# A decoder layer on one core: new orders on four engines, context remainders on VectorE, early loads of ScalarE's tables

## The reference

```
x = x + linear_attention(layernorm(x))            # 16 heads of 16; q, k -> elu + 1; kv = k^T v; (q kv) / (q sum(k) + 1e-6); o_w, o_b
x = x + softmax(mask(((ctx Wq)(ctx Wk)^T / 8) * layernorm(x)))    # ctx is 256 x 64; the "score" multiplies the normalised x
x = x + W_down(fwht(silu(gate) * up))             # up, gate = W_ug(fwht(layernorm(x))), 1024 wide each, with column scales
```

## Time and profile before

| | |
|---|---|
| three runs | 132.08, 132.26, 132.5 us; median 132.26 us |
| profiled execution, first to last instruction | 130.6 us (the profile gives no other time of its own for this execution) |
| PE busy | 123.9 us, 95% |
| PEld (weight loads, beside PE) | 116.0 us, 89% |
| DVE, ACT, POOL busy | 79.7, 75.4 and 68.8 us |
| granted TensorE clock | 1.000 |

### The profile page before, as it was taken

The page is one execution under the profiler, slowest core; times in us unless marked ns, Lnnn a source line. Parts: engine busy times, 40 slices in busy tenths (PEclk is TensorE's granted clock), DMA queues, the critical chain, the costliest instruction groups (busy, mean ns, idle before and its releaser), DMA issues.

```text
span 130.6 us, 2612 instructions
## 1 busy us (share of the span) xinstructions
PE 123.9 (95%) x974; PEld 116.0 (89%) x974; DVE 79.7 (61%) x202; ACT 75.4 (58%) x162; POOL 68.8 (53%) x89
## 2 busy tenths in 40 slices
PE   6899999996999999999999999999999999999991
PEld 2249799986999999699999999999999999999990
DVE  1279969677997794999786486662535512232211
ACT  1497639984576589668553883556496630345500
POOL 2200999889999998746270344452326350055500
PEclk9999999999999999999999999999999999999999
DMA  4999985000000000000000200000200000200011
GB/s 113 304 346 381 397 241 201 0 0 3 3 5 0 0 0 8 0 0 0 5 0 0 80 0 5 3 0 0 85 0 0 3 0 5 80 0 0 0 39 47
DMA packets 4353, 7.68 MB, mean 59 GB/s; under 512 B 560, under 2 KB 2096, under 8 KB 4212
## 3 DMA queue, kind: packets, MB, share of 16 engines
q1 hardware_dynamic: 4334, 7.50, 17.0%
q10 hardware_dynamic: 6, 0.01, 0.0%
HBM read 6.46 MB, written 1.05 MB: 57 GB/s over the span
## 4 chain that ended last, share of the span: by engine, by line
PE 60%; POOL 13%; DVE 11%; ACT 7%; issue 4%; DMA 3%; POOLq 0%; ACTq 0%
PE bank L1123 31%; PE bank L1136 18%; POOL wd_a L303 4%; POOL wug L309 4%; DMA x_res<-in_x 3%; PE bank L1003 3%; POOL rstd L263 2%; DVE st L644 2%; PE bank L1087 2%; PE bank L1109 2%; PE bank L1025 2%; POOL wd_b L303 2%; PE bank L1069 1%; ACT L518 1%; DVE xT L802 1%
## 5 line engine op out<-in xcount | busy, mean ns | idle before, releaser
L1123 PE MATMUL bank<-xh_home,wug 128*128 128x256 f32 x384 | 49.5, 285 | 0.3 <-DVE at L737 0.3
L1123 PEld LDWEIGHTS bank<-xh_home,wug 128*128 128x128 f32 x384 | 47.1, 191 | 0.9 <-issue 0.7
L314 POOL TENSOR_TENSOR hs<-front,hs 128x256 fp32r<-128x256 f32 x32 | 24.0, 758 | 33.1 <-ACT hs L527 33.1
L518 ACT ACTIVATE front<-bank,vecs 128x256 f32<-128x256 f32 x32 | 15.0, 472 | 20.3 <-PE bank L1123 20.1
L825 DVE SCALAR_TENSOR_TENSOR front<-bank,sc_up,front 128x256 f32<-128x256 f32 x32 | 15.2, 480 | 18.2 <-ACT front L518 18.2
L1136 PE MATMUL bank<-wdh,hs 128*128 128x256 f32 x192 | 23.7, 283 | 0.0
L1136 PEld LDWEIGHTS bank<-wdh,hs 128*128 128x128 f32 x192 | 23.3, 191 | 0.0
L527 ACT CAST hs<-front 128x256 fp32r<-128x256 f32 x32 | 12.8, 400 | 4.0 <-DVE front L825 4.0
L1025 PE MATMUL bank<-wqkv,xT 128*128 128x256 f32 x96 | 14.1, 288 | 0.1
L1025 PEld LDWEIGHTS bank<-wqkv,xT 128*128 128x128 f32 x96 | 12.2, 189 | 1.2 <-ACT xT L436 0.7
L261 POOL TENSOR_SCALAR veps<-mv 128x2 f32<-128x2 f32 x12 | 2.3, 192 | 19.8 <-DVE mv L647 19.1
(11 more groups left out here) (105 smaller groups left out, 194.1 us busy)
## 6 DMA issues: line engine op xcount, KB each, us to landing
wd_a<-in_w_d SPq DMA_DIRECT2D x1, 1024.0 KB, 8.6
front<-in_w_ug SPq DMA_DIRECT2D x2, 512.0 KB, 9.7
back<-in_w_ug SPq DMA_DIRECT2D x2, 512.0 KB, 5.0
out<-x_res SPq DMA_DIRECT2D x8, 128.0 KB, 1.9
wd_b<-in_w_qkv SPq DMA_DIRECT2D x3, 256.0 KB, 4.9
x_res<-in_x SPq DMA_DIRECT2D x1, 512.0 KB, 6.6
x_res<-in_x SPq DMA_DIRECT2D x1, 385.0 KB, 3.8
back<-in_ctx_t SPq DMA_DIRECT2D x1, 260.0 KB
```

The costliest lines, as they stand in the source:

```text
L314: g.tensor_tensor(hs[:, 1, n % JB, :], sg[:, n % RING, :], hs[:, 0, n % JB, :].bitcast(F32), ALU.subtract)\
L518: a.activation(sg[:, n % RING, :], B("GU", n)[:, 0:SEQ], ACT.Silu, scale=vecs[:, V_WSUG + JB + j:V_WSUG + JB + j + 1]).then_inc(s["sg"], 1)
L1123: ins = mm(dst[:, n * SEQ:(n + 1) * SEQ], wug[:, wa, k, at_col + j * P:at_col + (j + 1) * P], xh[b][:, xb, k, :], start=(i == 0), stop=(i ...
```

## The change

It alters no arithmetic. In its parts:

- `ctx_lo(0)` and `ctx_lo(1)`, the remainders of the context, go from POOL to DVE. The two subtractions keep their sizes, 65x256 and 65x512.
- POOL, ACT and DVE get new lists, written out call by call; PE gets new tables.
- On PE, SC(3) goes ahead of OUT(1) and SC(1) ahead of K(3); WD(3) and XH(1) come behind GU(6); NUM(3) moves into Y(0), between its two halves.
- ACT gets five instructions `table(f, n)`, an activation of one column with the function Exp or Silu; where the function differs from the one before, the table load comes with it.
- The semaphore `w_lo` becomes three, one for each weight.

The core of the diff (POOL's helper copies of `w_lo`, `wo_lo` and `scale_up` and DVE's of `add_ob` are never called and left out):

```diff
-        ("V", 2), ("SC", 2), ("AT", 1), ("Q", 2), ("T1", 3), ("OUT", 1), ("SC", 3), ("T3", 0), ("K", 3), ("SC", 1),
-        ("XH", 0), ("V", 3), ("Q", 3), ("ST", 2))
+        ("K", 2), ("NUM", 1), ("V", 2), ("SC", 2), ("AT", 1), ("Q", 2), ("T1", 3), ("SC", 3), ("OUT", 1),
+        ("T3", 0), ("SC", 1), ("K", 3), ("XH", 0), ("V", 3), ("Q", 3), ("ST", 2),)
...
-        (0, 4): (("AT", 2), ("WD", 2), ("WD", 3)), (0, 5): (("XH", 1),), (0, 7): (("OUT", 2),),
-        (1, 1): (("NUM", 3),), (1, 2): (("T3", 2),), (1, 3): (("AT", 3),), (1, 4): (("OUT", 3),), (1, 6): (("XH", 2),),
+        (0, 4): (("AT", 2), ("WD", 2),), (0, 6): (("WD", 3), ("XH", 1),), (0, 7): (("OUT", 2),),
+        (0, JB): (("NUM", 3),), (1, 2): (("T3", 2),), (1, 3): (("AT", 3),), (1, 4): (("OUT", 3),),
...
+            def table(function, n):
+
+                a.activation(table_in[:, n:n + 1], neg1[:, :], function)
...
+            exp_q(3)
             prob(1)
-            ug_hi(3)
-            exp_q(3)
+            table(ACT.Silu, 0)
+            pre_hi(0)
             negate_mean(3, 1)
-            pre_hi(0)
...
+            table(ACT.Exp, 1)
             prob(2)
+            silu(8)
+            table(ACT.Silu, 2)
             negate_mean(3, 2)
...
+            def ctx_lo(c):
+                cols = U_COLS[c]
+                dve.wait_ge(s["ctx_hi"], c + 1)
+                v.tensor_tensor(ctxr[:, 1, cols], ctxT[:, cols], ctxr[:, 0, cols].bitcast(F32), ALU.subtract)\
+                    .then_inc(s["ctx_lo"], 1)
```

More of the change, by code:

```diff
@@ L85, in schedule @@
         order += banks_of("Y", b)
[L86 removed]
+        order += [g for j in (JB, JB + 1, JB + 2) for name, i in SIDE.get((b, j), ()) for g in banks_of(name, i)]
     return [g for g in order if g not in (("SC", 0, 0), ("SC", 1, 0))]
@@ L568, in _ @@
             score_evac(3)
+            ug_hi(2)
             x3_hi(0)
+            xh_hi(0)
+            ug_hi(3)
             exp_k(3)
-            ug_hi(2)
-            xh_hi(0)
+            exp_q(3)
             prob(1)
-            ug_hi(3)
-            exp_q(3)
+            table(ACT.Silu, 0)
+            pre_hi(0)
             negate_mean(3, 1)
-            pre_hi(0)
[L578 to L595, removed]
@@ L596, in _ @@
-            h_hi(JB - 1)
+            pre_hi(1)
+            silu(0)
+            silu(1)
+            normalise(3, 1, xn3)
+            x3_hi(1)
+            h_hi(0)
+            h_hi(1)
+            silu(2)
+            silu(3)
+            h_hi(2)
+            silu(4)
+            wd_hi(0)
+            wd_hi(1)
+            at_hi(2)
+            h_hi(3)
+            silu(5)
+            wd_hi(2)
+            h_hi(4)
+            silu(6)
+            h_hi(5)
+            wd_hi(3)
+            xh_hi(1)
@@ L597, in _ @@
+            silu(7)
+            h_hi(6)
+            h_hi(7)
+            table(ACT.Exp, 1)
             prob(2)
+            silu(8)
+            table(ACT.Silu, 2)
             negate_mean(3, 2)
[L599 to L610, removed]
@@ L611, in _ @@
-            h_hi(2 * JB - 1)
+            normalise(3, 2, xn3)
+            silu(9)
+            silu(10)
+            h_hi(8)
+            x3_hi(2)
+            h_hi(9)
+            silu(11)
+            at_hi(3)
+            h_hi(10)
+            h_hi(11)
+            silu(12)
+            silu(13)
+            h_hi(12)
+            silu(14)
+            h_hi(13)
+            xh_hi(2)
+            silu(15)
+            h_hi(14)
+            table(ACT.Exp, 3)
+            h_hi(15)
             prob(3)
+            table(ACT.Silu, 4)
@@ L629, in _ @@
-            h_hi(4 * JB - 1)
+            silu(16)
+            silu(17)
+            h_hi(16)
+            normalise(3, 3, xn3)
+            silu(18)
+            silu(19)
+            h_hi(17)
+            h_hi(18)
+            x3_hi(3)
+            silu(20)
+            h_hi(19)
+            h_hi(20)
+            xh_hi(3)
+            silu(21)
+            silu(22)
+            h_hi(21)
+            silu(23)
+            h_hi(22)
+            h_hi(23)
+            silu(24)
+            silu(25)
@@ L633, in _ @@
+            h_hi(24)
+            h_hi(25)
+            silu(26)
+            h_hi(26)
+            silu(27)
+            silu(28)
+            h_hi(27)
+            silu(29)
+            h_hi(28)
+            silu(30)
+            h_hi(29)
+            h_hi(30)
+            silu(31)
+            h_hi(31)
         @block.vector
@@ L846, in _ @@
             v_add(0)
+            u_lo(0)
             u_lo(1)
+            ctx_lo(0)
             ln_stats(1, 2)
             scale_up()
+            xT_lo(1)
             elu_q(0)
-            xT_lo(1)
-            dve.wait_ge(ld["cst"], 16)
+            dve.wait_ge(ld['cst'], 16)
             diagonal(0)
@@ L860, in _ @@
             xT_lo(2)
-            elu_q(1)
+            ctx_lo(1)
+            v_add(1)
             add_attn(0)
             ln_stats(2, 0)
+            elu_q(1)
             diagonal(1)
```

229 lines of the change are left out of this document (132 added, 97 removed), and 3 rows, old and new, of tables (HEAD, SIDE).

## The result

The changed kernel takes 130.88 us (median of 130.48, 130.81, 130.95 and 133.37), the kernel before on the same chip 132.2 us (132.08 to 132.5). The ratio is 0.988, 95% interval 0.9844 to 0.9915. Run again in five rounds it took 130.27 us (129.91 to 130.96) against 132.4, ratio 0.9846 (0.9797 to 0.9894). The profiled execution of the changed kernel took 130.48 us with a span of 128.7 us, at a granted clock of 1.000; 130.3 and 128.65 had been predicted.

What follows compares the result with a forecast made beforehand. TensorE, busy 123.9 of 130.6 us, bounds the kernel; only its waits can be gained. Terms +0.25 - 1.25 - 0.2 - 0.35 - 0.3 - 0.1 = -1.95 us give 130.3 us; range 129.1 to 131.9 us (8 in 10).

Steps and rivals of the forecast that it cites:

- The lock and AT(0), +0.25 us: Head up to AT(0): `wo_lo`, with two SBUF operands, waits for POOL's first butterfly, so AT(0) starts 0.25 us later.
- AT(1), -1.25 us: AT(0) to gate stage: POOL's scale of norm 2 comes in time, `logits(0)` no longer delays `attend(1)`; 1.25 us gained.
- NUM(1), -0.2 us: Between AT(0) and the gate stage: 0.15 of NUM(1)'s 0.34 us loss stays, a gain of 0.2 us.
- The gate stage, -0.35 us: `attend(2)` ahead of `pre_lo(1)` more than covers 0.55 us at GU(4), less 0.2 us waiting at T3(1).
- -0.55 for GU(4): Gate stage: GU(4)'s 0.55 us wait for the bank that `attend(2)` frees goes.
- +0.2 us for T3(1): Gate stage: T3(1) waits 0.2 us, as `normalise(3, 1)` stands behind two `silu` and both `pre_hi`.
- The close race: Gate stage: `pre_lo(0)` on DVE taken to start before `ug_lo(3)` on POOL; estimates 1.3 against 1.28 us behind the statistics.
- the lost race: Rival at `pre_lo(0)`: `ug_lo(3)` runs first, GU(3) waits for its bank, costing 1.3 us; 131.6 us, chance 0.22.
- AT(3), -0.3 us: After the gate stage: NUM(3) goes into Y(0), so `attend(3)` is done well ahead of AT(3); 0.3 us gained.
- Fewer changes of operand, -0.1 us: Between GU steps on TensorE: fewer changes of operand gain 0.1 us.
- a DVE that starves between back-to-back POOL instructions: Rival at `wo_lo`, then `pre_lo(0)`: VectorE cannot get in between gapless POOL instructions; +1.75 us, 134.0 us, chance 0.11.
- the no-lock rival: Rival at `wo_lo`: it gets in ahead of or beside the butterfly; a further -0.9 us, 129.4 us, chance 0.18.

Runs made afterwards that it cites:

- `wo_lo` early: Changed kernel with `wo_lo` moved ahead of `elu_q(0)` and `diagonal(0)` on DVE; median 131.12 us.
- `wo_lo` from PSUM: Changed kernel with the first operand of `wo_lo` read from the PSUM bank of SC(0) instead of SBUF; median 130.15 us.
- `attend(2)` back: Changed kernel with `pre_lo(1)` ahead of `attend(2)` again on DVE; median 131.57 us, ratio to before 0.9932.
- `attend(2)` alone: Kernel before with only `hidden(1)` and `attend(2)` moved ahead of `pre_lo(1)` on DVE; ratio 1.0052.

## Why the prediction was right

The forecast, 130.3 us, lies between the two medians of the changed kernel in the table (130.81 and 130.27), and the sum of -1.95 us met -1.9 to -2.0 at the last matmul. Term by term, from the table and the timelines:

- *The lock and AT(0), +0.25 us.* Measured +0.25 (12.86 - 12.61; +0.14 in the second profile). `wo_lo` took 2.41 us and ended 0.55 behind the first butterfly, as stated, and `scale_up`, with POOL idle beside it, lasts 0.14 us instead of 0.71. The run with the operand from PSUM shows that the two SBUF operands are the cause. The Trainium skill ("SBUF — State Buffer", section "SBUF: two separate sides") has whichever starts first, such an instruction or a GpSimd one that reads SBUF, hold a shared pair of ports for its whole length, and these runs agree: 0.68 against 2.41 us.
- *AT(1), -1.25 us.* Measured -1.24: AT(1) follows NUM(1) by 3.14 us, in before by 4.38. The wait was the right one. VectorE's `logits(0)`, then GpSimd's shift of batch 3, in before:

```profile
30.09 0.49 DVE L770 CUSTOM_DVE_ANT_0 bank<-bank,mbias,rstd 128x256 f32<-128x256 f32 x1 [1.35 <-POOL rstd L263]
```

```profile
26.48 0.20 POOL L270 TENSOR_TENSOR nmr<-nmean,rstd 128x2 f32<-128x2 f32 x1 [0.61 <-ACT nmean L384]
```

In before `logits(0)` waits 1.35 us for POOL's scale of norm 2, in the changed kernel not at all. The reason given, the 1.96 us that POOL gives away, is only a part: with the subtractions back on POOL, `logits(0)` waits 0.58 us, not 1.35. Another part is the 0.61 us that POOL stood still in before for ACT's mean of batch 3, which ACT now makes ahead of the masks' bias. How the 1.24 us divide among the moves on POOL, ACT and DVE was not tried and stays open.

- *NUM(1), -0.2 us.* Wrong: it waits 0.17 us as before, and it follows AT(0) by 6.93 us, in before by 6.88. From AT(1) to GU(0), where no change was forecast, 0.06 us is gained (12.68 to 12.62).
- *The gate stage, -0.35 us.* Measured -0.69 (GU(0) to AT(2): 11.15 before, 10.46 after). The term was mis-sized: -0.55 for GU(4) was about right (GU(4) follows GU(3) by 2.44 us, in before by 3.06), and the +0.2 us for T3(1) didn't come. The prediction saw `normalise(3, 1)` behind both `pre_hi`, and let the table loads run "in ACT's idle time, for batches 2 and 3 as before"; it gave no value to the early load for batch 1, which alone is worth 0.9 us, and without which T3(1) does wait, 0.52 us.
- *The close race.* Taken as won, and it was, 48.24 against 48.34. That was in part luck: the reason given, that the shift ahead of `ug_lo(3)` must first get past `pre_lo(0)`, did not hold. The shift began 0.05 us ahead of `pre_lo(0)` and lasted its usual 0.19 us; `ug_lo(3)` came 1.28 us behind the statistics, as estimated, and `pre_lo(0)` 1.18, where 1.3 had been estimated. The price of the lost race was too low, 1.9 to 2.1 us where 1.3 had been worked out: GU(3) alone lost 1.8 us, as TensorE's slack there was 0.8 us and not 1.0 and `pre_lo(0)` came 2.6 us later and not 2.3, and `pre_lo(1)`, which then collides as well, cost another 0.25.
- *AT(3), -0.3 us.* The size is right, -0.29 (13.16 to 12.87 from Y(0) to AT(3)), the reason is not: with NUM(3) back the gain stays, and without the table columns too (12.86). The traces put it down to the move of `silu(8)` and its table load on ACT, which in before was not in idle time; that move by itself was not undone, so this is argued and not shown.
- *Fewer changes of operand, -0.1 us.* Not found: from AT(3) to the last end 50.36 us before, 50.43 after.

Of the rivals, a DVE that starves between back-to-back POOL instructions is refuted by `wo_lo` getting in between the two butterflies. The price of the no-lock rival was too high: without the lock the end came 0.4 to 0.55 us earlier, not 0.9, because AT(0) gains 0.7 to 0.8 and part of that is given back behind it.

The total came out closer than its parts, and that is luck: the missing 0.2 at NUM(1) and 0.1 of operand changes are made up by 0.35 us more in the gate stage, 0.2 of it the wait at T3(1) that the early table load saved.

## What to carry to other kernels

Where VectorE works on two SBUF operands next to long GpSimd instructions, read both timelines together: an instruction that lasts longer than its like was, in every case looked at here, one that waited, and which of the two is first can decide as much as the whole change (here 0.1 us of order against 2 us of time). A gain at one step is only what is left of it at the next shared release: of 0.8 us won at AT(0), half, nothing or less than nothing was left, by how it was won. Cost a table load by where it falls: of 1.28 us, none was lost in ACT's idle time, and 0.9 us of the end where `silu` and a normalisation stood behind it.

## What the runs showed of the hardware

In most profiles the span ends 2.7 to 2.8 us behind the last matmul; in those of `wo_lo` early, `wo_lo` from PSUM, `attend(2)` back and `attend(2)` alone it is 3.6 to 4.3 us. The DMA view of the last 6 us, from 125 us on in 40 slices of 0.15 us, for `wo_lo` early and then for the changed kernel again (us to landing at the end):

```profile
GB/s 0 0 0 0 0 0 0 0 109 0 164 328 280 48 0 0 0 0 14 7 7 14 14 0 0 0 0 0 0 0 0 0 0 0 0 0 0 0 0 0
...
q8 instruction: 1, 0.02, 1.5%
...
out<-x_res SPq DMA_DIRECT2D x1, 128.0 KB, 3.2
```

```profile
GB/s 41 0 0 0 0 0 0 0 0 0 0 89 341 328 116 0 0 0 0 0 0 0 0 0 0 0 0 109 0 0 0 0 0 0 0 0 0 0 0 0
...
out<-x_res SPq DMA_DIRECT2D x1, 128.0 KB, 1.8
```

In the first the output of 128 KB leaves a remnant at a low rate that lands 3.2 us after its issue instead of 1.8, and just ahead of it stands an instruction fetch of 16 KB (the 109 at 126.2 us). In the second that fetch, with its 109, comes at 129.2 us, when the output is done. In all four profiles with the long end the fetch falls on or just ahead of the last output, in the others earlier or later, and the two profiles of the changed kernel have it at different times (123.5 and 129.2 us). That the fetch causes the delay is inferred from this agreement; no run was made to test it. It may also be why the times of `wo_lo` early fall into two groups some 1.3 us apart; only one of those executions has a trace, so this stays open.
